# A fused attention and gated FFN kernel on one core: a new order for its prologue, K norm by halves, and a late last up projection

## The reference

```python
xn = _layernorm(x)                         # x: 1 x 1024 x 512, no weights
q = (xn @ Wq.T)  -> 32 heads x 1024 x 128;  k, v = xn @ Wk.T, xn @ Wv.T -> 8 heads
q = _rmsnorm(q, q_norm_w);  k = _rmsnorm(k, k_norm_w)
scores = q k^T / sqrt(128) + slope(head) * (key - query), causal
s = (softmax(scores) @ v -> 1024 x 4096) @ Wo.T
g = silu( (silu(xn @ gate) * (xn @ up)) @ down )   # int4 weights, scales and zeros by 128, inner size 1792
return x + s * g
```

## Time and profile before

| | |
|---|---|
| median of 3 runs | 1333.64 us (1332.92 to 1333.79) |
| profiled execution: time | 1337.71 us |
| profiled execution: span | 1335.5 us |
| TensorE busy | 1284.6 us (96%) |
| VectorE, ScalarE, GpSimd busy | 976.8, 649.4, 751.5 us |
| stages | prologue to 42.67 us, heads to about 1093 us, FFN to the end |

### The profile page before, as it was taken

One profiled execution on the slowest core, in us unless ns is written; L12 is line 12 of the kernel. 1 busy time (PEld: TensorE's weight loads), 2 busy tenths in 40 slices (PEclk: granted clock), 3 DMA queues, 4 the chain that ended last, 5 costly groups with the idle time before them and its releaser, 6 DMA issues. The chain is left out here.

```text
span 1335.5 us, 20919 instructions
## 1 busy us (share of the span) xinstructions
PE 1284.6 (96%) x7120; PEld 1103.6 (83%) x7120; DVE 976.8 (73%) x2067; ACT 649.4 (49%) x1420; POOL 751.5 (56%) x730
## 2 busy tenths in 40 slices
PE   5799999999999999999999999999999989999996
PEld 5688888888888888888888888888888878888884
DVE  5677787787778777877787778777888844555556
ACT  2555555556555555555555555555555523222222
POOL 3745575557555655565566556555565625555553
PEclk9799999999999999999999999999999999999998
DMA  3000000010000000100010000000020035444431
GB/s 120 16 17 17 33 16 17 17 32 17 16 17 32 17 17 16 33 16 17 17 32 17 17 17 33 17 17 16 17 70 18 1 112 160 134 129 130 129 104 63
DMA packets 29467, 57.87 MB, mean 43 GB/s; under 512 B 3648, under 2 KB 3648, under 8 KB 29248
## 3 DMA queue, kind: packets, MB, share of 16 engines
q1 hardware_dynamic: 29376, 56.68, 14.5%
HBM read 54.57 MB, written 2.10 MB: 42 GB/s over the span
## 5 line engine op out<-in xcount | busy, mean ns | idle before, releaser
L390 POOL TENSOR_TENSOR pb<-rel,coef 128x1024 f32<-128x1024 f32 (+7 forms) x256 | 298.3, 1183 | 94.9 <-PE T L845 89.9
L479 ACT ACTIVATE pb<-pb,low 128x1024 f32<-128x1024 f32 (+7 forms) x256 | 198.8, 777 | 188.0 <-DVE low L652 186.9
L469 ACT ACTIVATE pt_h<-T 128x512 fp32r<-128x512 f32 (+3 forms) x384 | 185.8, 486 | 123.1 <-PE T L845 119.9
L636 DVE TENSOR_TENSOR pt_l<-T,pt_h 128x512 fp32r<-128x512 f32 (+3 forms) x384 | 210.1, 549 | 43.2 <-ACT pt_h L469 41.9
L652 DVE CUSTOM_DVE_ANT_0 pb<-S,pb,ninv 128x1024 f32<-128x1024 f32 (+7 forms) x256 | 207.4, 810 | 38.3 <-PE S L867 33.2
L845 PE MATMUL T<-ident,pb 128*128 128x128 f32 x1152 | 191.8, 276 | 19.4 <-DVE pb L661 13.0
L845 PEld LDWEIGHTS T<-ident,pb 128*128 128x128 f32 x1152 | 142.3, 142 | 60.1 <-DVE pb L661 20.4
L661 DVE TENSOR_SCALAR pb<-pb,rinv 128x1024 f32<-128x1024 f32 (+7 forms) x256 | 170.6, 666 | 9.0
L864 PE MATMUL S<-kT_h,q_h 128*128 128x512 f32 (+2 forms) x384 | 142.8, 372 | 2.7 <-DVE kT_l L724 2.7
L368 POOL TENSOR_TENSOR root<-ms,cst 128x4 f32<-128x4 f32 x64 | 76.3, 1193 | 117.1 <-DVE ms L684 117.1
L883 PE MATMUL O<-pt_h,v_h 128*128 128x512 f32 (+2 forms) x384 | 140.7, 366 | 1.0 <-DVE pt_l L636 1.0
(11 more groups left out here) (138 smaller groups left out, 2931.4 us busy)
## 6 DMA issues: line engine op xcount, KB each, us to landing
wq_in<-in_wq SPq DMA_DIRECT2D x32, 256.0 KB, 2.8
wo_in<-in_wo SPq DMA_DIRECT2D x32, 256.0 KB, 2.6
stage<-in_wkv SPq DMA_DIRECT2D x8, 512.0 KB, 4.2
stage<-in_gate_w SPq DMA_DIRECT2D x14, 256.0 KB, 2.6
stage<-in_gate_z SPq DMA_DIRECT2D x14, 256.0 KB, 3.5
stage<-in_gate_s SPq DMA_DIRECT2D x14, 256.0 KB, 4.9
stage<-in_up_w SPq DMA_DIRECT2D x14, 256.0 KB, 5.3
stage<-in_up_z SPq DMA_DIRECT2D x14, 256.0 KB, 6.2
```

Source lines behind the costliest of these rows:

```text
L390: g_.tensor_tensor(pbuf(idx, t), rel[:, TOK - w:TOK], coef[:, t:t + 1].to_broadcast([P, w]), ALU.mult).then_inc(bias_ready, 1)
L469: a_.activation(pt_lot(pt_h, t, n), bank[:, 0:m * P].rearrange("p (k w) -> p k w", w=P), ACT.Copy).then_inc(tr_hi, 1)
L479: a_.activation(pbuf(idx, t), pbuf(idx, t), ACT.Exp, bias=low[:, idx:idx + 1], scale=-1.0, accum_out=rsum[:, idx:idx + 1]).then_inc(exps_r ...
L636: v_.tensor_tensor(pt_lot(pt_l, t, n), bank[:, 0:m * P].rearrange("p (k w) -> p k w", w=P), f(pt_lot(pt_h, t, n)), ALU.subtract).then_inc( ...
```

## The change

- TensorE first runs 14 matmuls on zeros (VectorE clears 640 columns of `pt_h` for them) into a bank that is overwritten later, one more between the LN transposes of tiles 0 and 1, and three behind them.
- LayerNorm goes by pairs of tiles: four powers of two columns instead of two of four. GpSimd, not VectorE, scales the tiles. The LN transposes of tiles 2 to 7 stand inside kv0, kv1 and kv2.
- The first load of `wkv_in` is issued by ScalarE at the start, not by SyncE behind four x tiles. Its high and low parts are made by halves.
- `qc1_0` stands ahead of `kv3`. K's mean square, norm and transposes go by halves, in group 0 also its splitting. In steady groups the first half of `k_norm` stands at the third head.
- The KV projection `kv0` for group 1 moves from the end of head 0 to between `qc0_0` and the second scores of head 0; its weights' low part is made by VectorE.
- `norms`: the root is the mean square times its inverse root (a product instead of a second power), behind a wait for it.
- The clearing of `s_acc` goes; the first output projections are copied there.
- FFN: the last up projection (c = 1) stands behind the down units 0 to 2 of the last step; three silus and three products come ahead of the last `hidden`. silu writes to PSUM.

```diff
-PRO = ["kv0", "kv1", "kv2", "kv3", "qc1_0"]
+PRO = ["kv0", "kv1", "kv2", "qc1_0", "kv3"]
@@ SyncE
-            if i == CT - 1:
-                sp.dma_start(wkv_in[:, :, :], wkv[0]).then_inc(wkv_ld, 16)
@@ GpSimd, norms(h, c)
-            g_.tensor_tensor(root[:, cs], ms[:, cs], half(1), ALU.pow).then_inc(root_ready, 1)
             g_.tensor_tensor(inv[:, cs], ms[:, cs], half(0), ALU.pow).then_inc(root_ready, 1)
+            pool.wait_ge(root_ready, n * 2 + 1)
+            g_.tensor_tensor(root[:, cs], ms[:, cs], inv[:, cs], ALU.mult).then_inc(root_ready, 1)
+            g_.tensor_tensor(ninv[:, cs], inv[:, cs], half(2), ALU.mult).then_inc(coef_ready, 1)
             pool.wait_ge(root_ready, n * 2 + 2)
-            g_.tensor_tensor(ninv[:, cs], inv[:, cs], half(2), ALU.mult).then_inc(coef_ready, 1)
@@ GpSimd, prologue
+        def ln_rows(n):
+            ts = slice(2 * n, 2 * n + 2)
+            pool.wait_ge(ln_var, n + 1)
+            g_.tensor_tensor(rstd[:, ts], var_e[:, ts], cst[:, 0:1].to_broadcast([P, 2]), ALU.pow).then_inc(ln_rstd, 1)
+            pool.wait_ge(ln_rstd, n + 1)
+            for i in (2 * n, 2 * n + 1):
+                g_.tensor_scalar(xs[:, i, :], xs[:, i, :], mv[:, i, 0:1], rstd[:, i:i + 1], ALU.subtract,
+                                 ALU.mult).then_inc(xn_ready, 1)
+        wkv_lo_half(0)
+        ln_rows(0)
+        wkv_lo_half(1)
+        ln_rows(1)
+        ln_rows(2)
+        ln_rows(3)
         wq_lo(0)
-        pool.wait_ge(tr_ready, QT)
-        g_.memset(s_acc[:, :], 0.0).then_inc(sT_zero, 1)
-        k_norm(0)
+        k_norm(0, 0)
         norms(0, 1)
+        k_norm(0, 1)
@@ GpSimd, heads
                 bias(h, 5)
+                if j == 2 and not last:
+                    k_norm(g + 1, 0)
                 bias(h, 6)
...
                 if j == PER - 1 and not last:
-                    k_norm(g + 1)
+                    k_norm(g + 1, 1)
@@ ScalarE, prologue
-        wkv_hi_part(0)
+        act.dma_start(wkv_in[:, :, :], wkv[0]).then_inc(wkv_ld, 16)
+        act.wait_ge(wkv_ld, 16)
+        for n in range(2):
+            ks = slice(2 * n, 2 * n + 2)
+            a_.activation(wkv_h[:, ks, :], wkv_in[:, ks, :], ACT.Copy).then_inc(wkv_hi, 1)
         wq_hi_part(0)
+        ln_hi(range(0, 5))
+        k_squares(pro, ["kv0"], 0)
+        ln_hi(range(5, 7))
+        k_squares(pro, ["kv1"], 0)
+        ln_hi(range(7, 8))
@@ VectorE, prologue
+        first_kv_copy(3)
+        k_mean_sq(0, 1)
+        dve.wait_ge(wkv_hi, 3)
+        v_.tensor_tensor(wkv_l[:, :, :], wkv_in[:, :, :], f(wkv_h[:, :, :]), ALU.subtract).then_inc(wkv_split, 1)
@@ TensorE, prologue
+        pe.wait_ge(warm, 1)
+        idle_matmuls(14)
         pe.wait_ge(setup, SETUP + 5)
+        ln_transposes(0)
+        idle_matmuls(1)
+        ln_transposes(1)
+        idle_matmuls(3)
+        for n in range(3):
+            kv_proj(pro, f"kv{n}", 0, {6: [lambda n=n: ln_transposes(2 * n + 2)], 18: [lambda n=n: ln_transposes(2 * n + 3)]})
+        pe.wait_ge(tr_lo, QT)
         q_proj(pro, "qc1_0", 0)
+        kv_proj(pro, "kv3", 0, {4: [lambda: first_k_transposes(0)],
+                                14: [lambda: squares(pro.hi("qc1_0"), 1, QT, T[1])]})
@@ TensorE, group 0
-                q_proj(at, "qc0_0", 0, {9: [lambda: squares(pro.hi("qc1_0"), 1, QT, T[1])]})
-            k_transposes(g)
+                q_proj(at, "qc0_0", 0)
+                def first_scores():
+                    pe.wait_ge(kt_lo, 2)
+                    scores(0, 0)
+                kv_proj(at, "kv0", 1, {6: [lambda: first_k_transposes(1)], 20: [first_scores]})
@@ FFN: VectorE and TensorE, the last step
-        for n in range(4):
+        for n in range(7):
             last_add(n)
+        for n in range(3):
+            times_s(n)
         hidden(IT - 1, 1)
-        for n in range(4, 16):
+        for n in range(7, 16):
             last_add(n)
-            if 9 <= n < 13:
-                times_s(n - 9)
+            if n == 8:
+                times_s(3)
...
-        gate_up(IT - 1, 1, 1)
-        y_units(IT - 1, 1, range(0, 4), place=4)
+        gate_up(IT - 1, 1, 1, kinds=("gate",))
+        y_units(IT - 1, 1, range(0, 3), place=4)
+        gate_up(IT - 1, 1, 1, kinds=("up",))
+        y_units(IT - 1, 1, range(3, 4), place=7)
```

More of the change, by code:

```diff
@@ L123, in group_order @@
         out += [f"qc0_{j}"] + [f"v0_{j}"] * prev + [f"w0_{j}", f"w1_{j}"] * w
-        out += [f"qc1_{nx}"] * more + [f"w2_{j}"] * w + [f"kv{j}"] * (not last)
+        if first and j == 0:
+            out += ["kv0", "qc1_1"]
+        else:
+            out += [f"qc1_{nx}"] * more + [f"w2_{j}"] * w + [f"kv{j}"] * (not last)
         out += [f"v1_{j}"] + [f"w3_{j}"] * w
@@ L426, in group @@
                 bias(h, 3)
-                if j == 0 and not last:
+                if j == 0 and not last and kind != "first":
                     wkv_lo(g + 1)
@@ L539, in group @@
                     exp(h, 0)
-                elif kind != "last":
+                elif kind == "steady":
                     wkv_hi_part(g + 1)
                 q_hi(at, f"qc0_{j}")
+                if kind == "first" and j == 0:
+                    act.wait_ge(kt_ready, 2)
+                    kT_hi_part(0, slice(CH, TOK))
                 if j == 0:
@@ L743, in group @@
                     q_lo(at, f"qc0_{j}")
+                elif kind == "first":
+                    q_lo(at, f"qc0_{j}")
+                    dve.wait_ge(kt_hi, 2)
+                    kT_lo_part(slice(CH, TOK))
+                    logits(h, 0)
+                    logits(h, 1)
                 else:
@@ L757, in group @@
                 if w:
-                    project(at, f"w0_{j}", unit)
+                    project(at, f"w0_{j}", unit, kind == "first")
                 normalise(h, 2)
+                if j == 2 and not last:
+                    k_mean_sq(g + 1, 0)
                 lot(h, 6, 0)
                 if w:
-                    project(at, f"w1_{j}", unit + 1)
+                    project(at, f"w1_{j}", unit + 1, kind == "first")
                 lot(h, 6, 1)
@@ L768, in group @@
                 logits(h, 4)
+                if kind == "first" and j == 0:
+                    kv_copy(at, ["kv0"], 1)
                 if more:
@@ L779, in group @@
                 normalise(h, 5)
-                if not last:
+                if not last and (prev or j > 0):
                     kv_copy(at, [f"kv{j}"], g + 1)
@@ L913, in kv_proj, with k_transposes, first_k_transposes @@
             ins.then_inc(out_ready, 1)
-        def k_transposes(g):
-            pe.wait_ge(kn_ready, g + 1)
-            if not (isinstance(g, int) and g == 0):
-                pe.wait_ge(logits_ready, g * (PER * QT) - 1)
-            for k in range(QT):
+        def k_transposes(tiles):
+            for k in tiles:
                 ins = nc.tensor.transpose(S[0][:, k * P:(k + 1) * P], kv[:, k, 0:HD], ident[:, :])
             ins.then_inc(kt_ready, 1)
+        def first_k_transposes(c):
+            pe.wait_ge(kn_ready, c + 1)
+            k_transposes(range(c * CT, (c + 1) * CT))
         def project(at, name, unit, h0, j0, outputs):
@@ L1210, in _ @@
         step(IT - 1, 1, last=True)
[L1211 to L1214 removed]
+        for n in range(3, UNITS):
+            silu_y(n)
     @block.vector
```

203 lines of the change are left out of this document (115 added, 88 removed).

## The result

| | before | changed |
|---|---|---|
| median | 1333.72 us (4 runs, 1332.92 to 1335.13) | 1325.27 us (4 runs, 1325.12 to 1325.52) |
| profiled execution: time, span | 1337.71, 1335.5 us | 1325.52, 1323.4 us |

The ratio is 0.9932, with a 95% interval from 0.9919 to 0.9945: 8.45 us faster. I had forecast 1317 us, with a range of 1311 to 1324; the time lies outside it, 1.3 us above its upper end.

A forecast was written before the change was run, and what follows sets the result against it. TensorE was busy 96% of the span, so gains lay in its waits, half clock and the end. From the profiled 1337.71 us, -9.2 - 2.5 - 5.2 = -16.9 gave 1320.8; less 4.07, about 1317 us, range 1311 to 1324.

The forecast's parts named there:

- wait for w_l: Near 37 us, kv0 for group 1 waits for VectorE's low part of its weights: a stall of 2.1 us.
- A scaled tile on GpSimd: LayerNorm at the start: GpSimd scales one x tile in 1.0 us, bounded by 0.8 and 1.54 us.
- a sign of being wrong: Head 0: the forecast was to count as wrong if PEclk is at 0.50 there.
- a rival at 17%: Head 0: VectorE's split and scalings meet GpSimd's biases, the clock halves, half the gain is lost: 1320 to 1324 us, 17%.
- The new start does nothing, as x tiles behind wkv come too late: Rival on the start: only steady groups and the end gain, 1326 us; needs the last tile 8 us later; 4%.
- the last line of the sum: Profile to median: 4.07 us taken off 1320.8, as the profiled execution stood that far above its median, giving 1316.7.
- -2.8 and -0.3: Head 0: us saved because its query projection and what precedes it run at full instead of half clock.
- start to the first scores of head 1: The new start and head 0 together: first scores of head 1 9.2 us earlier, at 65 instead of 74.43 us.
- The end: FFN's last step: adds, silus and products fill VectorE's 4.75 us hole; last sum at 1327.7 instead of 1333.03, -5.2 us.
- The steady groups: Group starts: GpSimd is 2.4 us earlier, so seven waits of 0.33 us go, with 0.4 at heads 1 and 2: -2.5.
- The slower rival: Every head: GpSimd's biases, 0.8 us earlier, meet VectorE's scalings and TensorE waits; at 0.8 us a head 1342 us; 4%.
- kv0 to the first scores: Start: kv0 from 13.0 us, some 4 us at half clock, qc1_0 at 27.0, first scores at 41.0 instead of 42.67.

The follow-up runs named there:

- e1: The changed kernel, but VectorE instead of GpSimd scales the eight x tiles, in pairs; GpSimd keeps the powers: 1319.70 us.
- e4: The changed kernel without its 18 idle matmuls: 1324.23 us.
- e6: e1 without the 18 idle matmuls: 1321.85 us.
- e8: e1 with the high and low parts of group 1's KV weights made by halves: 1320.41 us.
- e10: e1 with the first two xh ahead of wq_h, and the first pair scaled ahead of the second variance: 1321.60 us.
- e11: e10 with the first KV weights loaded by SyncE behind two x tiles, and GpSimd's first power ahead of their low part: 1322.43 us.
- e12: e1 with x ahead of the KV weights, the first two xh ahead of wq_h, and VectorE's list in the order its results are asked for: 1318.65 us.
- e5: The kernel before with the new norms, K's mean square and norm by halves, and the new end, but the old start and head 0: 1325.95 us.
- e9: The changed kernel itself measured again, on another chip: 1324.04 us, ratio 0.9919 to the kernel before.
- e2: The kernel before with only the new FFN part: 1331.19 us against 1335.68.
- e7: The changed kernel with norms making the root by a second power again, K's norm still by halves: 1330.93 us.

## Why the prediction was wrong

The forecast stood on a chain of places. They can be read off one by one:

| place | forecast | changed | e1 |
|---|---|---|---|
| last scaled tile ready | 20.1 | 29.05 | 19.17 |
| kv0 starts | 13.0 | 15.29 | 14.11 |
| qc1_0 starts | 27.0 | 31.18 | 26.39 |
| wait for w_l | 2.1 | 1.21 | 1.21 |
| first scores | 41.0 | 44.91 | 40.13 |
| first probability transposes | 46.5 | 50.53 | 45.74 |
| first scores of head 1 | 65 | 71.71 | 65.45 |

**The term that was mis-sized** is "A scaled tile on GpSimd", with 1.0 us, "from above 1.54 us, the mean of the first four biases". It measured 2.07 us, outside my bounds: eight of them are 8.6 us of the 8.95 by which the last tile is late. The bounds came from instructions of one operation; this one has two. The first half of K's scaling did land where I put it (1.04 us for 512 columns); the second took 1.74, beside VectorE's subtraction for `w_l`. With that term replaced by VectorE's 0.50 to 0.79 us (e1) every place from `qc1_0` on comes within 0.9 us of the forecast. e1 gives back 6.3 of the 6.5 us that were missing at the first scores of head 1. The Trainium skill's page "GPSIMD Engine Reference", section "Elementwise — side-by-side cycle accounting", has its 2.6 cycles for `tensor_tensor`, not for this operation. My estimate of 1.1 us from it is no better here: the row shows 1.9 times that.

Part of this agreement is luck. Stage by stage, e1 against the forecast: up to `kv0` +1.1 us, since the first x tile came at 5.6 us and not at 4.2, and VectorE, busy without a gap from then on, made the first `xl` at 13.28; `kv0` to `qc1_0` -1.7; to the first scores -0.3; to the first probability transposes +0.1; from there to the first scores of head 1 +1.0. The stretches that I mis-sized cancel to 0.2 us.

**The clock in head 0** is the other part of the miss. The changed kernel took 21.2 us from the first probability transposes to the first scores of head 1, where I had 18.7 and e1 took 19.7: 1.5 of the 6.5 us are lost there, where the clock was at half from 51.96 to 58.79 us. e4, at half for 3.1 us (56.5 to 59.6) in which TensorE had no gap, took 21.3; the six kernels that kept the clock in head 0 (e1, e6, e8, e10, e11, e12, which also all scale on VectorE) took 19.7 each. I had named this as a sign of being wrong, and it is in a rival at 17%. But VectorE was not held there: its first long scaling took 0.75 us, not 2.40. The 2.40 us on which I built that rival I had also misread. GpSimd's biases were over at 48.11 us (41.94 and 6.17), and the scaling began at 48.56. What ran beside it in the kernel before was the subtraction for the KV weights, which the change gives to VectorE:

```profile
48.06 2.34 POOL L351 TENSOR_TENSOR w_l<-stage,w_h 128x1024 fp32r<-128x1024 f32 x1
```

Another of my rivals had this outcome: "The new start does nothing, as x tiles behind wkv come too late", 1326 us, "It needs the last tile 8 us later than I have it". The tile was 8.95 us later, and e5 shows the start to be worth next to nothing. Only its reason was another: the tiles did not arrive late but were scaled late. I gave it 4% because I had bounded a price for which I had no row by rows of another kind.

**The second error** is the last line of the sum. I took 4.07 us off the forecast because before's profiled execution stood that far above its median. The 47 runs of before show that this was its scatter, which goes with the clock, from 1332.1 to 1339.5 us, and its profiled execution (1337.71, clock 0.992) was one of the slower group. The new kernels scatter less, e9's and e1's profiled executions lie within 1.6 and 0.5 us of their medians, and my sum had already taken the half clock in head 0 out of the profiled execution (-2.8 and -0.3). The same microseconds were taken off twice. Measured 0.25 us, not 4.07, lay between the changed kernel's profiled execution and its median.

**The account** in us from the unrounded 1316.7: start to the first scores of head 1 +6.5 (-2.7 for -9.2); heads and FFN up to the last step -1.8 (1229.7 for 1234.0, so -4.3 for -2.5); the end +0.1 (22.0 for 27.0, -5.1 for -5.2); time beside the span -0.1; profile to median +3.8. Sum 1325.2; measured 1325.27.

**What held.** The end, by e2: 4.5 us in the medians, 5.1 within the span. Two small errors cancel in it: from `hidden` to the last sum 0.5 us less than I had, and from there to the last store 3.3 us where before had 2.47. The steady groups' sign and place: the wait of 0.33 us at the group's start is gone, the list of waits shrank from 9.1 to 6.1 us. Its size was too small, since I counted the group starts and left out the other halves of heads in which the power stands; e7 gives 5.7 us for the power by itself. ScalarE waited for wq until 11.0 us as forecast, and in e1 that held the first `xh`; in the changed kernel ScalarE then stood idle for 0.59 us more, waiting for TensorE's transposes of the tile. The slower rival (biases 0.8 us earlier meet VectorE's scalings) did not come: the waits for such scalings fell. Of "kv0 to the first scores", the clock at half for some 4 us was 6.8 us in the changed kernel and 3.4 in e1; in head 0 it fell in the changed kernel (51.96 to 58.79) and not in e1, e6 or e12, although the waits there are much the same: 1.82 and 1.1 us in the changed kernel, 1.8, 1.4 and 0.5 in the others. What decides it there stays open.

## What to carry to other kernels

Before an operation is moved to another engine, look for a row there with the same number of operations and operand kinds, and where none exists let the upper bound be the sum of two single operations (here twice 1.04 to 1.29 us, which takes in the 2.07), then ask what the chain does at that bound. A step meant to keep an engine's clock up, or to start it early, is worth something only once the producer behind it is no longer the bound: the same 18 idle matmuls brought nothing that could be told in one kernel and gained 2.15 us in another. When a profiled execution differs from the median, compare the mean clock of the runs before subtracting the difference from a forecast that already counts on the clock.

## What the runs showed of the hardware

- GpSimd: `tensor_scalar` with two operations and two operands by partition, 128x512 f32, 2.07 us, eight times alike, with VectorE busy for 44 to 63% of that time; VectorE 0.50 alone, up to 1.0 a tile beside a GpSimd subtraction (e11). GpSimd's `tensor_tensor` for K's scaling, 128x512 f32, 1.04 us, and 1.74 beside a VectorE subtraction. GpSimd's powers: 0.72 us for two columns (three of the four in e1 0.92 to 0.93), 1.01 for four, 1.64 for eight.
- The transfer of the KV weights, started beside x, moved the first x tile from 3.51 to 5.74 us; issued behind two tiles of x (e11) it left the first at 3.37 and put the third at 7.9 us, where the kernel before had it at 5.5.
- The time of the kernel before moves by up to 7 us from run to run, and the mean clock of a run, printed to three digits, tells which group it is in. In every profiled execution of this case TensorE works at half clock in the first 62 us only; for the runs without a profile this is not shown. The mean clock is a rough guide: it leaves out half clock ahead of the first change in the record (e6 has 0.999, though it works at half until 19.3 us), and it counts the fall behind the last matmul, which costs nothing (in before's profiled execution from about 1326 us to the end).
